# Two-layer gated attention with routed experts on one core: ranks ahead of attend, one scatter a slot, identity products between the layers, mask bias by quadrants

## What is computed

```python
scores = jnp.einsum('bhqd,bhkd->bhqk', q, k)
scores = jnp.where(m == 0, -1e9, scores) / jnp.sqrt(D_K)
ctx = jnp.einsum('bhqk,bhkd->bhqd', jax.nn.softmax(scores), v)

x = x + tanh(g_xattn[0]) * xattn0(layernorm(x), ctx, mask)
x = x + tanh(g_ffn[0])   * experts_top1_of_8(layernorm(x))       # 512 hidden, gelu
x = x + tanh(g_xattn[1]) * xattn1(layernorm(x), ctx)
x = x + tanh(g_ffn[1])   * experts_top2_of_16(x)                 # 64 hidden, silu, capacity 8
```

## Time and profile before

| | us |
|---|---|
| median of 3 executions | 534.26 |
| lowest, highest | 531.89, 535.05 |
| the profiled execution, its own time | 535.57 |
| its span in the trace | 533.6 |
| PE busy | 452.7 (85%) |
| DVE busy | 365.5 (68%) |
| ACT busy | 322.0 (60%) |
| POOL busy | 273.5 (51%) |

### The profile page before, as it was taken

One profiled execution on the slowest core, in us unless ns is written; L12 is line 12 of the kernel. 1 busy time (PEld: TensorE's weight loads), 2 busy tenths in 40 slices (PEclk: granted clock), 3 DMA queues, 4 the chain that ended last, 5 costly groups with the idle time before them and its releaser, 6 DMA issues.

```text
span 533.6 us, 19576 instructions
## 1 busy us (share of the span) xinstructions
PE 452.7 (85%) x7243; PEld 337.8 (63%) x7243; DVE 365.5 (68%) x977; ACT 322.0 (60%) x764; POOL 273.5 (51%) x325
## 2 busy tenths in 40 slices
PE   2789999998988896999985789988898777778887
PEld 1456776776776695999982466665565556444454
DVE  5678777978686857355542779889998786553455
ACT  2355565565765684677744566767667556775553
POOL 2522533556553347888886535353535316533455
PEclk9999999999999989799996799999999997899999
DMA  7114343232101134665445010110031000000112
GB/s 200 49 53 140 80 117 110 72 106 75 43 12 52 30 80 119 80 97 77 49 38 149 1 44 5 42 32 24 3 92 31 16 2 3 1 1 12 34 46 71
DMA packets 50620, 30.53 MB, mean 57 GB/s; under 512 B 12384, under 2 KB 46944, under 8 KB 50528
## 3 DMA queue, kind: packets, MB, share of 16 engines
q1 hardware_dynamic: 37072, 18.54, 12.9%
q0 software_dynamic: 6640, 4.67, 6.6%
q10 hardware_dynamic: 6816, 6.07, 4.0%
HBM read 19.41 MB, written 9.85 MB: 55 GB/s over the span
## 4 chain that ended last, share of the span: by engine, by line
PE 54%; DVE 14%; issue 13%; POOL 8%; ACT 6%; DMA 3%; ACTq 1%; DVEq 1%; SPq 0%; POOLq 0%
PE T_ps L861 8%; PE A_ps L876 7%; PE S_ps L850 7%; POOL x_mid L1140 6%; DVE maxes L603 5%; PE S_ps L844 3%; PE m_H_ps L1427 3%; PE Q_ps L831 2%; PE f_H_ps L1192 2%; PE m_T_ps L1467 2%; PE Q_ps L752 2%; PE m_X_ps L1454 2%; PE m_X_ps L1410 2%; PE X_ps L893 2%; PE Q_ps L763 2%
## 5 line engine op out<-in xcount | busy, mean ns | idle before, releaser
L603 DVE TENSOR_REDUCE maxes<-S_ps 128x8 f32<-128x512 f32 x128 | 87.6, 684 | 45.7 <-PE S_ps L850 45.6
L430 POOL TENSOR_TENSOR k_blk<-kT,col_a 128x512 f32<-128x512 f32 x64 | 67.7, 1068 | 86.2 <-ACT kT L491 59.7
L533 ACT ACTIVATE probT<-T_ps 128x512 f32<-128x512 f32 x128 | 76.0, 594 | 43.3 <-PE T_ps L861 42.8
L611 DVE TENSOR_TENSOR prob<-S_ps,maxes 128x512 f32<-128x512 f32 x128 | 88.5, 692 | 4.4
L861 PE MATMUL T_ps<-col_a,prob 128*128 128x128 f32 x512 | 83.2, 286 | 9.8 <-DVE prob L611 6.8
L861 PEld LDWEIGHTS T_ps<-col_a,prob 128*128 128x128 f32 x512 | 56.8, 143 | 47.1 <-issue 34.7
L1140 POOL DMA_INDIRECT x_mid<-f_out,f_rows x39 | 60.9, 1561 | 12.1 <-issue 10.7
L876 PEld LDWEIGHTS A_ps<-v_blk,probT 128*32 128x32 f32 (+1 forms) x3072 | 53.0, 119 | 10.6 <-issue 10.4
L876 PE MATMUL A_ps<-v_blk,probT 128*32 128x18 f32 (+1 forms) x3072 | 59.3, 195 | 0.0
L850 PE MATMUL S_ps<-k_blk,qT 32*64 32x256 f32 x1024 | 46.2, 415 | 5.4 <-DVE prob L611 2.9
L1005 DVE TENSOR_TENSOR f_hid<-f_H_ps,f_b 128x512 f32<-128x512 f32 x39 | 27.0, 692 | 33.3 <-PE f_Y_ps L1206 28.5
(11 more groups left out here) (198 smaller groups left out, 876.3 us busy)
## 6 DMA issues: line engine op xcount, KB each, us to landing
f_w<-in_W ACTq DMA_DIRECT2D x16, 256.0 KB, 2.8
ctxT<-in_ctxT SPq DMA_DIRECT2D x12, 256.0 KB, 3.1
f_rows<-sorted_rows SPq DMA_DIRECT2D x39, 64.5 KB, 2.0
out<-m_final SPq DMA_DIRECT2D x32, 64.0 KB, 1.5
x_all<-in_x SPq DMA_DIRECT2D x6, 256.0 KB, 5.0
x_mid<-x_all SPq DMA_DIRECT2D x6, 256.0 KB, 3.1
x_all<-x_mid SPq DMA_DIRECT2D x6, 256.0 KB, 3.7
ctxT<-in_ctxT SPq DMA_DIRECT2D x8, 128.0 KB, 2.6
```

Of the source, the lines that this page charges most:

```text
L430: nc.gpsimd.tensor_tensor(k_blk[:, t % 2, :, :, :], kT[:, g.at(R), t - g.first, :].rearrange("p (b k) -> p b k", b=2).unsqueeze(2).to_broa ...
L533: nc.scalar.activation(probT[:, t % 2, 4 * h:4 * h + 4, :], T_ps[:, :, :], ACT.Exp, scale=SCALE).then_inc(probT_ready, 1)
L603: nc.vector.tensor_reduce(maxes[:, t % 2, h, :, :], half_of(h), X, ALU.max).then_inc(max_ready, 1)
L611: nc.vector.tensor_tensor(prob[:, t % 2, heads, :].rearrange("p (r e) k -> p r e k", r=2), half_of(h), maxes[:, t % 2, h, :, :].unsqueeze( ...
```

## The change

1. `rank` and `rank_slots` stand behind `turn_probs(1)` and ahead of `attend` in PE's list; `keep_ranks` stands behind `exp(1)` in ACT's.
2. `scatter` of the first five groups issues one tile a slot, not two.
3. Identity products whose result nobody reads: eight of 512 columns into `S_ps[1]` among the projections ahead of layer 1, and two of 256 columns and one of 512 into `T_ps` in its first slots.
4. The mask lies on both partition halves: `mask_in[half, ..., u, b, :]` holds the rows of both sequences of a tile on each half, loaded by two DMAs per group. Each holds as many bytes as the one did. The conversion covers twice the columns. The bias is written by eight products of 64 rows x 64 columns of the array, 256 columns each, in place of four of 128x128. The rings hold two groups, not four; loads stand at 7 slots ahead and conversions at 2.

```diff
@@ attention, rings
-    mask_in = sb("mask_in", [P, R, Q, S], I32)
-    mask_bias = sb("mask_bias", [P, R, Q, S], BF16)
+    mask_in = sb("mask_in", [P, MR, Q, 2, S], I32)
+    mask_bias = sb("mask_bias", [P, MR, Q, 2, S], BF16)
...
@@ sync_steps, load_mask
+                if g.i >= MR:
+                    sp.wait_ge(mask_made, g.i - MR + 1)
+                for half in range(2):
+                    sp.dma_start(mask_in[half * S:(half + 1) * S, g.at(MR), 0:g.n, :, :].rearrange("q u b k -> q (u b) k"),
+                                 dram["mask"][dram_rows(g), :].rearrange("(m q) k -> q m k", q=S)).then_inc(mask_loaded[g.at(MR)], 16)
...
-                steps += [(load_mask, groups, head(-11)), (keep, groups, tail(5))]
+                steps += [(load_mask, groups, head(-7)), (keep, groups, tail(5))]
...
@@ gpsimd, scatter: slot of tile t
-... + (t - GROUP_OF[t].first) // 2)]
+... + (t - GROUP_OF[t].first) // (1 if GROUP_OF[t].own < LAST_GROUPS else 2))]
...
@@ vector, mask(g), and its place
+                wait(dve, scored, tiles_to(g.i - MR))
+                nc.vector.tensor_scalar(mask_bias[:, at, 0:n, :, :], mask_in[:, at, 0:n, :, :], 0.0, MASKED, ALU.is_equal, ALU.mult).then_inc(mask_made, 1)
...
-                ... (mask, groups, head(-4))]
+                ... (mask, groups, head(-2))]
...
@@ tensor_ahead
+        def stream_into(bank, n):
+            eye = w["ident"][:, :]
+            nc.tensor.matmul(bank[:, 0:n, :], eye, eye.unsqueeze(1).to_broadcast([P, n, P]), start=True, stop=True)
...
+            return [(project_k, early, k_ahead), (stream, early, k_ahead), (project_v, early_units, v_ahead), (stream, early_units, v_ahead),
+                    (stream, range(STREAMED), lambda n: 2 * NT)]
...
@@ score, layer 0
                     for h in range(2):
-                        for k in range(2):
-                            nc.tensor.matmul(S_ps[h][:, k, 0:HQ * S].rearrange("p (e k) -> p e k", k=S), w["ident_bf"][:, :],
-                                             mask_bias[:, g.at(R), u, :].unsqueeze(1).to_broadcast([P, HQ, S]),
-                                             start=True, stop=False, skip_group_check=True)
+                        for b in range(2):
+                            for k in range(2):
+                                rows, queries = slice(k * S, (k + 1) * S), slice(b * S, (b + 1) * S)
+                                nc.tensor.matmul(S_ps[h][queries, k, 0:HQ * S].rearrange("p (e k) -> p e k", k=S), w["ident_bf"][rows, rows],
+                                                 mask_bias[rows, g.at(MR), u, b, :].unsqueeze(1).to_broadcast([S, HQ, S]),
+                                                 start=True, stop=False, skip_group_check=True, tile_position=(k * S, b * S))
...
@@ tensor, list of steps
+            awake = [] if masked else [(lambda n: stream_into(T_ps, n), [Q // 2], lambda _, when=when: when) for when in (NT - 3.95, NT - 1.99)]
+            awake += [] if masked else [(lambda n: stream_into(T_ps, n), [Q], lambda _: NT - 1)]
+            steps = [score_ahead] + awake + [(turn_probs(1), tiles, shift(0)),
+                     (rank if masked else rank_slots, groups, settled(7 if masked else 8, 12, short, later)), (attend, tiles, shift(1)), ...
```

More of the change, by code:

```diff
@@ L102 @@
 SINGLY = 7
+STREAMED = 3
 F1_PARTS = 4
@@ L187, in attention @@
     XR = 3
+    MR = 2
     NR = 4
@@ L255, in attention @@
     ctx_loaded = [sem(f"ctx_loaded{k}") for k in range(CR)]
-    mask_loaded = [sem(f"mask_loaded{k}") for k in range(R)]
+    mask_loaded = [sem(f"mask_loaded{k}") for k in range(MR)]
     kept = [sem("kept_full"), sem("kept_rest")]
@@ L478, in gpsimd @@
             if masked:
-                steps += [(scatter, tiles, lambda t: settled(8 if GROUP_OF[t].own < 7 else 7, 13, short, later)(GROUP_OF[t]) + (t - GROUP_OF[t].first) // 2)]
+                steps += [(scatter, tiles, lambda t: settled(8 if GROUP_OF[t].own < 7 else 7, 13, short, later)(GROUP_OF[t]) + (t - GROUP_OF[t].first) // (1 if GROUP_OF[t].own < LAST_GROUPS else 2))]
             else:
@@ L589, in scalar @@
             k_out, v_out = scalar_steps(act)
-            steps = [(exp(1), tiles, shift(0)), (keep_logits, groups, settled(6, 9, short, later)), (avT_out, groups, tail(2)), (q_out, groups, head(-2)),
-                     (keep_ranks, groups, settled(7 if masked else 8, 12, short, later)), (v_out, late_units, unit_head(-1)), (k_out, late, head(-3)),
+            steps = [(exp(1), tiles, shift(0)), (keep_ranks, groups, settled(7 if masked else 8, 12, short, later)), (keep_logits, groups, settled(6, 9, short, later)), (avT_out, groups, tail(2)), (q_out, groups, head(-2)),
+                     (v_out, late_units, unit_head(-1)), (k_out, late, head(-3)),
                      (exp(0), tiles, shift(-1)), (r_xnT_out, groups, settled(5, 8, short, later)), (xnT_out, groups, turn_x_at), (normed, tiles, normed_at), (r_normed, units, lambda u: settled(4, 7, short, later)(u.group))]
@@ L654, in mask @@
             def mask(g):
[L655 to L658, removed]
+                n, at = g.n, g.at(MR)
+                dve.wait_ge(mask_loaded[at], 32 * (g.i // MR + 1))
+                wait(dve, scored, tiles_to(g.i - MR))
+                nc.vector.tensor_scalar(mask_bias[:, at, 0:n, :, :], mask_in[:, at, 0:n, :, :], 0.0, MASKED, ALU.is_equal, ALU.mult).then_inc(mask_made, 1)
             def choose(g):
@@ L736, in vector @@
             if masked:
-                steps += [(choose, groups, settled(6, 11, short, later)), (rows, groups, settled(7, 12, short, later)), (mask, groups, head(-4))]
+                steps += [(choose, groups, settled(6, 11, short, later)), (rows, groups, settled(7, 12, short, later)), (mask, groups, head(-2))]
             else:
@@ L767, in tensor_steps, with stream @@
             return project_k, project_v
+        def stream_into(bank, n):
+            eye = w["ident"][:, :]
+            nc.tensor.matmul(bank[:, 0:n, :], eye, eye.unsqueeze(1).to_broadcast([P, n, P]), start=True, stop=True)
         def tensor_ahead(pe):
             project_k, project_v = tensor_steps(pe, x_banks["q"])
-            return [(project_k, early, k_ahead), (project_v, early_units, v_ahead)]
+            def stream(_):
+                stream_into(S_ps[1][:, 0, :].rearrange("p (u k) -> p u k", k=P), Q)
+            return [(project_k, early, k_ahead), (stream, early, k_ahead), (project_v, early_units, v_ahead), (stream, early_units, v_ahead),
+                    (stream, range(STREAMED), lambda n: 2 * NT)]
         def tensor(pe):
@@ L896, in tensor @@
             score_ahead = (score, tiles, score_at)
-            steps = [score_ahead, (turn_probs(1), tiles, shift(0)), (attend, tiles, shift(1)), (logit, groups[:7], settled(6, 9, short, later)),
+            awake = [] if masked else [(lambda n: stream_into(T_ps, n), [Q // 2], lambda _, when=when: when) for when in (NT - 3.95, NT - 1.99)]
+            awake += [] if masked else [(lambda n: stream_into(T_ps, n), [Q], lambda _: NT - 1)]
+            steps = [score_ahead] + awake + [(turn_probs(1), tiles, shift(0)),
+                     (rank if masked else rank_slots, groups, settled(7 if masked else 8, 12, short, later)), (attend, tiles, shift(1)), (logit, groups[:7], settled(6, 9, short, later)),
                      (turn_av, groups, tail(2)), (project_q, groups, head(-2)), (output, groups, tail(3)),
                      (logit, groups[7:], settled(6, 9, short, later)),
-                     (rank if masked else rank_slots, groups, settled(7 if masked else 8, 12, short, later)), (project_v, late_units, unit_head(-1)), (project_k, late, head(-3)),
+                     (project_v, late_units, unit_head(-1)), (project_k, late, head(-3)),
                      (turn_probs(0), tiles, shift(-1)), (turn_r, groups, settled(5, 8, short, later)), (turn_x, groups, turn_x_at)]
```

## The result

The changed kernel takes 544.49 us (median of 10 runs, 537.61 to 551.38); the kernel before, on the same chip, 534.65 (10 runs, 531.89 to 537.36). The ratio is 1.012, with a 95% interval from 1.0085 to 1.0153: slower by about 1.2% (6.4 us), where 531.1 and "within 1%" were forecast. Every ratio here leaves out executions more than 1.5% above the fastest of their kernel, which the medians keep: of the changed kernel three of ten, at 548.96 to 551.38, and the median of the other seven is 540.71. The profiled execution took 543.86.

What follows compares the result with a forecast made beforehand. PE was taken to set the pace in layer 0's attention, PE and DVE in turn in layer 1. -1.0 - 2.1 - 0.6 + 0.5 = -3.2 us gave a median of 531.1 us, range 526.5 to 537.5.

Steps and rivals of the forecast that it cites:

- The sign: Whole kernel: the change was forecast to make it faster, by 3.2 us in sum.
- Mask conversion, loads, scatters: Layer 0: DVE's doubled conversion costs +0.5 us where DVE doesn't wait; moved loads and single scatters cost or win nothing.
- Quadrants: Layer 0's mask products: eight 64x64 in two rounds save 0.04 to 0.08 us a tile, -1.0 us with weight loads.
- Rival 1: Mask products: half of what the changes of form cost is hidden, -6.4 in place of -1.0, 525.7 us; chance 0.17.
- rivals 2 and 3: Mask products: same-row pairs don't overlap, +4.5, 536.6 us, chance 0.11; no overlap at all, +18.2, 550.3 us, chance 0.06.
- Ranks first: Rank products ahead of attend: -2.3 us of avT waits, +0.7 for late `chosen`, -0.5 in layer 1; sum -2.1.
- Rival 5: Ranks first is paid for by waits for `chosen`: upper bound +2 us, 535.2; chance 0.12.
- Identity products: Between the layers: they hold PE's clock up, so layer 1's second score is faster; -0.6 us for all.
- the second score at 0.69 us: Layer 1's second score: at 2.4 GHz it takes 0.69 us in place of 1.16, -0.5 us.
- Single scatters: Layer 0, first five groups: one scatter a slot takes bursts off POOL; nothing won, nothing lost.
- Rival 4: Between the layers: identity products hold PE at a low clock and delay turn_x; +4 us, 535.7; chance 0.07.

Runs made afterwards that it cites:

- e2: Kernel before with only the mask conversion moved from 4 slots ahead to 2: 545.45 us, ratio 1.019.
- e8: Changed kernel with the mask conversion back at 4 slots ahead: 532.25 us, ratio 0.994 of the kernel before.
- e14: Changed kernel with the conversion at 4 slots ahead and the ranks back behind `output`: 531.18 us, ratio 0.987 of the kernel before.
- e5: Kernel before with quadrant products, doubled mask, two-group rings and loads at 7 slots, conversion at 4: 534.92 us, ratio 1.000.
- e11: e14 with all eight mask products of each tile issued twice: 537.31 us, ratio 1.002 of the kernel before.
- e12: e10 without the identity products (quadrants, conversion at 4, single scatters, ranks behind): 531.80 us, ratio 0.990 of the kernel before.
- e3: Kernel before with ranks first alone, in PE's and ACT's lists: 534.02 us, ratio 0.999.
- e10: Changed kernel with the conversion at 4 and the ranks back behind `output`: 531.93 us, ratio 0.992 of the kernel before.
- e9: Changed kernel with the mask conversion at 3 slots ahead: 536.37 us, ratio 0.996 of the kernel before.
- e17: The same program as e14, run again (changed kernel, conversion at 4, ranks behind): 530.84 us, ratio 0.992 of the kernel before.

## Why the prediction was wrong

The sign was wrong. The step that failed is "Mask conversion, loads, scatters". It priced the conversion as DVE work ("twice the columns are at most 7.6", "+0.5") and said of the load that it waits for the conversion, but put no price on the conversion's own move from 4 slots ahead to 2. The later place adds a wait of PE for DVE, and I never asked where DVE stands when PE wants the mask. The trace of before held the answer, PE first, then DVE:

```profile
117.38 0.60 PE L844 MATMUL S_ps<-mask_bias,ident_bf 128*128 128x256 bf16 x4
```

```profile
118.96 0.94 DVE L672 TENSOR_TENSOR r_chosen<-r_level,r_first 128x32 bf16<-128x32 f32 x1
119.83 0.15 DVE L641 SCALAR_TENSOR_TENSOR shift_by<-stats,rstd 128x2 f32<-128x2 f32 x1
```

At 2 slots ahead the conversion stands between these two rows of DVE, at 119.83, and ends some 0.4 later; the score that needs it starts at 117.38. That is a wait of 2.9 us. (It was 2.10 in e2 and 2.21 in the changed kernel: the 0.94 of `r_chosen` is another operation beside a k_blk of POOL, at 118.81 for 1.05 us, and takes 0.19 in the changed kernel.) An estimate made in hindsight, half of 2.9 on average over seven groups, would have put the step at about +10, the sum at about +7, and the forecast near 541. Measured were 9.7 us of waits in seven places and 1.0 in an eighth; the late conversion alone costs 1.9% (e2, 10.2 us), the other edits give some 3 us back (e8), and the whole is +6.4 us by the ratio. The +9.8 us between the medians holds three executions at 549 to 551 besides, and that it comes so near the 9.7 is chance. The +0.5 that the step did charge, for a longer conversion, wasn't there: 3.8 us, as before.

Point by point:

- Quadrants, -1.0: the form and its overlap were right, the size was too small. The mask group is 0.34 (0.36 forecast) and the added change of form 0.09 (0.14 and 0.03 forecast), so 0.10 a tile, 3.2 us over 32. Where the score waits for DVE's subtraction, the transposes' share is hidden and 0.19 shows: a light tile's step fell from 4.27 to 4.08 us. By tile 15, ahead of the scatters' effect, e14 was 2.07 us ahead, and by tile 31 e5 3.10. Rival 1 (pays in full) was half right in mechanism, rivals 2 and 3 (no overlap) are out by e11.
- The total does not show this alone (e5: 1.000, with an interval to 0.996), and together with single scatters it does (e12: 0.990).
- Ranks first, -2.1: the exchange was seen and its balance misjudged. Three waits of 0.77 went and two of 2.0 us together came (e3), in layer 1 1.5 us went and 2.5 came; the total didn't move. Rival 5's mechanism is what happened; its size, +2, did not. With single scatters beside it layer 0 gains 1.3 us (e8 against e10), an interaction that the sum, which adds the four edits, has no term for.
- Identity products, -0.6: "the second score at 0.69 us" was wrong, it takes 1.16. The clock held through PE's wait of 2.50 us and the transposes behind it, and fell about the next wait, ahead of the score. That x arrives late and the first maximum stands behind shift_by was right.
- Single scatters, 0: wrong. I looked at who waits for k_blk and not at what else POOL's pair of k_blk stands beside. It is worth 1.6 us in one slot; what it is worth in the total is not shown.
- Rival 4 (identity products in the way) did not occur: `turn_x` waited for xn, not for PE's order.

A version faster than both kernels came out: the changed kernel with the conversion at 4 slots ahead and the ranks back, 0.987, 0.992 and 0.992 of before in three sessions (531.18, 531.93 and 530.84 us).

## What to carry to other kernels

When an operation is moved in an engine's order, price its place before its size: read at what time its engine passes the new place, and when its reader wants the result. Two rows of the old trace give that, and here they outweigh every other term. A preparation that costs 0.4 us can cost 2 us of the bounding engine a group if it stands behind the slot's work. And a wait that is removed is only won if what stands next in line isn't late as well: in ranks first and in the identity products it was.

## What the runs showed of the hardware

- Two VectorE comparisons of 16 columns took 1.02 and 0.97 us, and one 2.10, beside GpSimd products of 1.03 us each (0.17 to 0.18 without), while a reduction with one input took its 0.17 beside such a product. A tiny operation can last as long as the neighbour's large one.
- Eight 64x64 products of 256 columns in bf16, in pairs on the same rows, cost 0.22 us when added to eight others (e11), and a change of form 0.09 to 0.12.
- TensorE worked at the full clock through its identity products (1.00 in 278 to 302 us), then stood 2.50 us, did its transposes still at the full clock (0.66 us), stood 0.76 us, and its next score ran at the low level (1.16 for 0.69).
- Mean clock differs between executions of one program: 0.94 to 0.976 in e9, whose times run from 528.8 to 541.8 us. In one stretch, 150 to 187 us, two profiles of one program have 0.77 (e14) and 0.96 (e17). A single execution tells nothing of half a per cent.
